# A packed second map in layer 0, its low part cut in three on VectorE, and other places for the degree counts

## The reference

```
x = layernorm(x + L0(x))     # L0: h = rmsnorm(x)*w; c = h@W_root + b + sum_r mean_r(h[src]@W_rel[r]);  r = 0, 1;  286 columns
                             #     L0 = x + elu(c) @ wo,   wo is 286 x 1024
x = layernorm(x + L1(x))     # L1: u = x@root + b + sum_r mean_r(x[src]) @ weight[r];  r = 0..7;  1024 x 1024 each
                             #     z = [u, x] @ w_gate + b;  L1 = tanh(u)*z + x*(1-z)
```

## Time and profile before

| | before |
|---|---|
| time, three runs | 837.8 us median (837.72 to 839.01) |
| profiled execution, its own time | 838.67 us |
| its span in the trace | 836.9 us |
| PE busy | 818.8 us, 98% |
| DVE busy | 672.2 us, 80% |
| ACT busy | 438.3 us, 52% |
| granted TensorE clock | 0.999 |

### The profile page before, as it was taken

How to read it: one execution, slowest core, us unless ns; L and a number is a source line. 1 busy time by engine, 2 the same in 40 slices (tenths; PEclk the granted TensorE clock), 3 DMA queues, 4 the chain that set the end, 5 groups by cost and what they waited for, 6 DMA issues and landing times.

```text
span 836.9 us, 15905 instructions
## 1 busy us (share of the span) xinstructions
PE 818.8 (98%) x6326; PEld 586.5 (70%) x6326; DVE 672.2 (80%) x969; ACT 438.3 (52%) x606; POOL 14.3 (2%) x32
## 2 busy tenths in 40 slices
PE   6999999999999999999999999999999999999996
PEld 5566744458877868768677686776867868778544
DVE  8999698998978677687776777767678676788997
ACT  5888558376556254453554535535456254444711
POOL 1000000000000000000000000000000000000000
PEclk9999999999999999999999999999999999999999
DMA  9411369202220220202202112021120220305711
GB/s 314 111 31 27 128 226 223 105 1 101 102 101 1 101 102 1 100 3 97 100 0 100 30 70 100 0 100 58 42 100 0 100 91 11 126 2 152 201 51 73
DMA packets 60125, 70.82 MB, mean 85 GB/s; under 512 B 30663, under 2 KB 34371, under 8 KB 60084
## 3 DMA queue, kind: packets, MB, share of 16 engines
q1 hardware_dynamic: 59207, 69.39, 26.2%
q10 hardware_dynamic: 876, 0.85, 0.4%
HBM read 57.71 MB, written 5.18 MB: 75 GB/s over the span
## 4 chain that ended last, share of the span: by engine, by line
PE 89%; DVE 6%; ACT 3%; DMA 1%; issue 1%; SPq 0%; DVEq 0%; ACTq 0%
PE psP L1162 51%; PE psA L1233 21%; PE psP L982 12%; PE psA L971 2%; PE psP L1086 1%; PE psP L942 1%; ACT cu_mem L676 1%; DVE p_mem L1463 1%; PE psP L991 1%; DVE vec L1384 1%; ACT wsplit L709 1%; DVE p_mem L1462 1%; DMA stage<-in_src 1%; ACT dump L596 0%; DVE wsplit L1410 0%
## 5 line engine op out<-in xcount | busy, mean ns | idle before, releaser
L1162 PE MATMUL psP<-wsplit,xT 128*128 128x256 f16 x2592 | 294.6, 273 | 0.0
L1162 PEld LDWEIGHTS psP<-wsplit,xT 128*128 128x128 f16 x2592 | 253.6, 98 | 33.0
L1233 PE MATMUL psA<-p_mem,cu_mem 128*128 128x512 f16 x800 | 175.3, 379 | 0.0
L1162 PE MATMUL psP<-wsplit,x 128*128 128x256 f16 x1296 | 150.3, 273 | 0.0
L1233 PEld LDWEIGHTS psA<-p_mem,cu_mem 128*128 (+1 forms) x800 | 78.2, 98 | 91.1 <-DVE cu_mem L1722 0.3
L1162 PEld LDWEIGHTS psP<-wsplit,x 128*128 128x128 f16 x1296 | 126.8, 98 | 14.6
L1424 DVE SCALAR_TENSOR_TENSOR wsplit<-stage,sc,wsplit 128x1024 f16<-128x1024 f32 x90 | 114.7, 1279 | 26.9 <-ACT wsplit L671 26.9
L671 ACT ACTIVATE wsplit<-stage,sc 128x1024 f16<-128x1024 f32 x90 | 100.6, 1137 | 16.6 <-DVE sc L1302 10.6
L1722 DVE SCALAR_TENSOR_TENSOR cu_mem<-psA,coef,cu_mem 128x512 f32<-128x512 f32 x80 | 60.0, 750 | 31.4 <-PE psA L1233 30.0
L671 ACT ACTIVATE wsplit<-x,sc 128x1024 f16<-128x1024 f32 x54 | 61.8, 1144 | 41.6 <-PE psP L1162 31.0
L1424 DVE SCALAR_TENSOR_TENSOR wsplit<-x,sc,wsplit 128x1024 f16<-128x1024 f32 x54 | 69.2, 1282 | 10.2 <-ACT wsplit L671 9.8
(11 more groups left out here) (211 smaller groups left out, 791.8 us busy)
## 6 DMA issues: line engine op xcount, KB each, us to landing
stage<-in_L_gnn_weight SPq DMA_DIRECT2D x16, 2048.0 KB, 7.8
stage<-in_L_gnn_w_gate SPq DMA_DIRECT2D x4, 2048.0 KB, 8.1
x_home<-x SPq DMA_DIRECT2D x5, 512.0 KB, 3.8
x<-x_home SPq DMA_DIRECT2D x5, 512.0 KB, 5.6
x<-in_x SPq DMA_DIRECT2D x4, 512.0 KB, 9.0
xT<-in_L_gnn_root SPq DMA_DIRECT2D x1, 2048.0 KB, 9.0
stage<-in_L_gnn_root SPq DMA_DIRECT2D x1, 2048.0 KB, 8.3
out<-x SPq DMA_DIRECT2D x4, 512.0 KB
```

Source lines behind the costliest of these rows:

```text
L1162: last = nc.tensor.matmul(psP[:, bank, (col + tt) * FB:(col + tt + 1) * FB], lhs[tt](a, c), split_block(n, b)[:, c, :], start=(first and t ...
L1233: last = nc.tensor.matmul(psA[:, (NT * h + t) % 2, :], cnt8[:, r, s, t * P:(t + 1) * P], p_part[h][a][:, s, :], start=(s == 0 and a == 0), ...
```

## The change

- wo's last chunk has only 30 rows. It is now packed: the rows are loaded three times, at partitions 0, 32 and 64 (three DMAs); wo's high part keeps all three, and its low part overwrites partitions 32 to 63. y's columns 256 to 285 are written three times at the same distances, and after the transposes y's low part overwrites partitions 64 to 93. So one matmul with 96 rows gives the three products of the chunk: 7 matmuls for a half and not 9 (`packed_product`).
- `wo_high` and `wo_low` go by chunks (three instructions each), `wo_low` now stands ahead of the layer 0 coefficients on DVE, and wo's scale ahead of the last `first_sums`. The second half of root, which waits for `wo_lo`, may load from then on.
- y's scaling goes from DVE (L1612, one a tile) to ACT (`y_scaled`, two a tile), with a shift from DVE. Row factors are made for tiles 0 and 1, 2 and 3, and 4, in three groups and not two. `y_low` is two instructions a tile and not one.
- On PE the degrees of layer 1 are counted in two pieces of 100: ahead of `wo_product(0)` and behind `root_product(0)`. `turn_y` of tiles 0 and 1 stands in the middle of `aggregate0` of tile 4. `aggregate0(0)` waits for the last sums only at its last source tile.
- Banks: three of the ten `wo_product` halves go elsewhere (halves 7 and 8 to psA), and `root_product(t)` writes bank (t + 3) % 5, the ones whose adds come first.
- On DVE root's low blocks 0 to 2 and 3 stand ahead of `x1_low(0)`, and `y_low(4)` and `wo_add(1, 0)` behind it. On ACT `y_high(4)` stands behind the first square root.

```
         def wo_bank(n):
+            return (psP[:, n, :] if n < NT else
+                    (psP[:, 0, :], psP[:, 1, :], psA[:, 1, :], psA[:, 0, :], psP[:, 2, :])[n - NT])
+        def root_bank(t):
+            return psP[:, (t + 3) % NT, :]
...
-            sp.dma_start(st_wo[0:F - (FC - 1) * P, FC - 1, :], wo_d[(FC - 1) * P:F, :]).then_inc(wo_tail_loaded, 16)
+            for q in range(3):
+                sp.dma_start(st_wo[q * QUAD:q * QUAD + FREST, FC - 1, :], wo_d[(FC - 1) * P:F, :]).then_inc(wo_tail_loaded, 16)
...
-            sp.wait_ge(wo_lo, 1)
+            sp.wait_ge(wo_lo, FC)
             load(U_ROOT + 1, 1, by_chunk(root_d[:, HALF:D]))
...
+            def y_scaled(t):
+                act.wait_ge(y_factors, t // 2 + 1)
+                last = elu_tmp[:, t, F - FREST:F].unsqueeze(1).broadcast_to([P, 2, FREST])
...
+                nc.scalar.activation(twice, last, ACT.Identity, bias=y_shift[:, t:t + 1], scale=rows_f[:, 0, 2, t:t + 1])
+                nc.scalar.activation(acc0[:, t, 0:F], elu_tmp[:, t, :], ACT.Identity, bias=y_shift[:, t:t + 1],
+                                     scale=rows_f[:, 0, 2, t:t + 1]).then_inc(y_ready, 1)
-            for t in range(NT - 1):
-                elu_exponential(t)
+            elu_exponential(0)
+            elu_exponential(1)
+            weight_sum(U_ROOT, 0, slot_load(U_ROOT), parts=(0,))
+            y_scaled(0)
+            y_scaled(1)
+            elu_exponential(2)
+            elu_exponential(3)
             y_high(0)
             y_high(1)
-            weight_sum(U_ROOT, 0, slot_load(U_ROOT), parts=(0, 1))
+            weight_sum(U_ROOT, 0, slot_load(U_ROOT), parts=(1,))
+            y_scaled(2)
             elu_exponential(NT - 1)
+            y_scaled(3)
             weight_sum(U_ROOT, 0, slot_load(U_ROOT), parts=(2, 3))
+            y_scaled(4)
             y_high(2)
             y_high(3)
             raw_high(U_ROOT, 0)
-            y_high(4)
...
+            def packed_product(out, t, cols):
+                _, hi, lo = unit_weights(U_WO)
+                for c in range(FC - 1):
+                    for a, w, first in ((0, hi, c == 0), (0, lo, False), (1, hi, False)):
+                        nc.tensor.matmul(out, yT[:, a, c, bass.ts(t, P)], w[:, c, cols], start=first, stop=False)
+                return nc.tensor.matmul(out, yT[0:3 * QUAD, 0, FC - 1, bass.ts(t, P)], hi[0:3 * QUAD, FC - 1, cols],
+                                        start=False, stop=True)
...
+            WO_FREE = {NT: (wo_added, 1), NT + 1: (wo_added, 2), NT + 2: (y_lo, 4), NT + 3: (y_lo, 5), NT + 4: (wo_added, 3)}
...
             def y_low(t):
                 dve.wait_ge(y_hi, t + 1)
-                tt(yT[:, 1, :, t * P:(t + 1) * P], psA[:, t % 2, 0:FPAD].rearrange("p (c n) -> p c n", c=FC),
-                   yT[:, 0, :, t * P:(t + 1) * P], ALU.subtract).then_inc(y_lo, 1)
+                nodes, third = slice(t * P, (t + 1) * P), slice(2 * QUAD, 3 * QUAD)
+                tt(yT[:, 1, 0:FC - 1, nodes], psA[:, t % 2, 0:FPAD - P].rearrange("p (c n) -> p c n", c=FC - 1),
+                   yT[:, 0, 0:FC - 1, nodes], ALU.subtract)
+                tt(yT[third, 0, FC - 1, nodes], psA[third, t % 2, FPAD - P:FPAD], yT[third, 0, FC - 1, nodes],
+                   ALU.subtract).then_inc(y_lo, 1)
...
             wo_add(0, 0)
+            unit_scale(U_ROOT, 0)
             wo_add(0, 1)
-            raw_low(U_ROOT, 0, (0, 1))
+            y_low(2)
+            y_low(3)
+            raw_low(U_ROOT, 0, (0, 1, 2))
             x1_factors(0)
+            raw_low(U_ROOT, 0, (3,))
+            x1_low(0)
             y_low(4)
             wo_add(1, 0)
-            x1_low(0)
             wo_add(1, 1)
-            raw_low(U_ROOT, 0, (2, 3))
             x1_factors(1)
```

More of the change, by code:

```diff
@@ L632, in wo_high @@
                 act.wait_ge(w_used, 1)
-                st, hi, _ = flat_weights(U_WO)
-                nc.scalar.activation(hi, st, ACT.Copy, scale=sc_f[:, scale_col(U_WO, 1), 2:3]).then_inc(wo_hi, 1)
+                st, hi, _ = unit_weights(U_WO)
+                for c in range(FC):
+                    nc.scalar.activation(hi[:, c, :], st[:, c, :], ACT.Copy,
+                                         scale=sc_f[:, scale_col(U_WO, 1), 2:3]).then_inc(wo_hi, 1)
             def weight_sum(i, slot, loads, parts=range(4)):
@@ L651, in weight_sum, with raw_high @@
                                          accum_out=am[:, slot, n:n + 1]).then_inc(wsum_ready, 1)
-            def raw_high(i, slot):
+            def raw_high(i, slot, blocks=range(4)):
                 act.wait_ge(scale_step, 4 * i + 4)
-                for n, (k, f) in enumerate(RAW):
+                for n in blocks:
+                    k, f = RAW[n]
                     b = weight_blocks(i) + n
@@ L963, in count_any, with product @@
                             quad(b, q0 + p, False)
-            def product(out, lhs, i, t, cols, part=None):
+            def product(out, lhs, i, t, cols, part):
                 _, hi, lo = unit_weights(i)
-                chunks = FC if i == U_WO else DC
-                for c in part or range(chunks):
+                for c in part:
                     for a, w, first in ((0, hi, c == 0), (0, lo, False), (1, hi, False)):
                         last = nc.tensor.matmul(out, lhs[:, a, c, bass.ts(t, P)], w[:, c, cols],
-                                                start=first, stop=(c == chunks - 1 and a == 1))
+                                                start=first, stop=(c == DC - 1 and a == 1))
                 return last
+            def packed_product(out, t, cols):
[5 more added lines that the diff above has]
+                                        start=False, stop=True)
             def raw_product(out, lhs, i, t):
@@ L1581, in _ @@
                 onehot_any()
-            unit_scale(U_WO, 1)
+            for c in range(FC):
+                wo_low(c)
             dve.wait_ge(deg0_full, 1)
@@ new lines, in y_factor @@
+            def y_factor(t0, t1):
+                tiles = slice(t0, t1)
+                dve.wait_ge(elu_done, t1)
+                step(nc.vector.tensor_reduce(rowmax[:, 0, tiles], elu_tmp[:, tiles, :], AX.X, ALU.max))
+                row_scales([rows[:, 0, a, tiles] for a in range(4)], rowmax[:, 0, tiles].bitcast(I32), least=127)
+                ts(y_shift[:, tiles], rows_f[:, 0, 2, tiles], -1.0, None, ALU.mult).then_inc(y_factors, 1)
+                ts(cy[:, tiles], rows_f[:, 0, 3, tiles], sc_f[:, U_WO, 3:4], 0.5, ALU.mult, ALU.mult).then_inc(cy_ready, 1)
```

107 lines of the change are left out of this document (58 added, 49 removed).

## The result

| | before | changed |
|---|---|---|
| time, 11 runs each | 837.84 us median (837.66 to 839.01) | 840.19 us median (838.97 to 841.58) |
| ratio of medians | 1 | 1.0026, 95% interval 1.0017 to 1.0035 |
| profiled execution: time, span, clock | 838.67, 836.9, 0.999 | 838.99, 837.2, 0.996 |

Slower by 0.26%, where 2.7 us (0.3%) faster were forecast. Two differences must be explained: the profiled execution is 0.3 us slower, not 2.7 faster, and the median is 1.2 us above that execution. Four of the 11 executions took 838.97 to 839.32 us, with a clock of 0.996 over the whole run, and seven 840.08 to 841.58, with 0.994 or 0.992.

What follows compares the result with a forecast made beforehand. Bound: PE, busy 98%, with a close race of PE, DVE and ACT ahead of its unbroken run. The second root tile starting at 132.0, not 134.69, gives 2.7 us off the 837.8 median: 835.1, range 833.9 to 837.2.

Steps and rivals of the forecast that it cites:

- PE's work: Second map on PE: ten halves lose 2 matmuls each at 0.2156 us, 20 matmuls or 4.31 us.
- the sentence on the degrees: PE, layer 1 degrees: still 200 matmuls at 0.0252 us, 5.0 us, half of them now following the first root tile.
- ScalarE: Rival: ACT's scaling pairs step by 2.3 us, ACT becomes the bound, kernel slower at 841.2; chance 0.04.
- wo's split: ACT and DVE before layer 0 coefficients: 3.33 us leave DVE's path at 100.34, coefficients start 1.15 later, at 92.4.
- The scaling on ACT: y's scaling: DVE loses five at 0.367; ACT gains pairs of 0.63 and 0.43, stepping by 0.88, 4.4 us for five.
- The layout up to root tile 1: Hand-laid order of PE, ACT and DVE: second root tile starts at 132.0 instead of 134.69, 2.7 us gained.
- Layer 1 takes it over: After the root tiles: layer 1 keeps the 2.7 us lead, for which DVE must itself be 1.2 earlier.
- Given back in the chain: Rival: ACT and DVE chain, 107 to 128 us, gives most back; gain 0.9, 836.9; chance 0.20.
- root's second load: Rival: the load issued at 92.4 shares the first one's bandwidth, holding the first scaling; gain 1.7, 836.1; chance 0.03.
- the cheap matmul: Rival: removed matmuls cost 131 ns rather than 216, so the saving is 1.7 less, 836.8; chance 0.01.

Runs made afterwards that it cites:

- spread kernel: Changed kernel with only its degree matmuls moved on TensorE, into pieces of 50, 50 and four of 25 in place of two blocks of 100; median 837.26 us, ratio 0.9991.
- one slower record: The changed kernel itself, unaltered, profiled a second time; one execution, 840.81 us at a clock of 0.992.
- the filler: Changed kernel with the later 100 degrees moved ahead of tile 4 and 12 unused 512-column matmuls behind root tile 0; median 838.93 us, ratio 1.0010.

## Why the prediction was wrong

- **PE's work.** The matmul price was right, 7 matmuls a half at 0.2156, the 96-row one the same: a half steps by 1.52, 7 times 0.217. What was wrong is the sentence on the degrees. I priced 100 of them at 0.0252 each, 2.5 us, which is what the block took, and took its place behind root tile 0 as free but for that, in the gap ahead of tile 1. It cost 1.7 us more on the 216 matmuls behind it (48.47 us for 46.78), which the forecast took to run as before ("the same layer 1 from there"). **This is the step that failed**: the working has no term for the clock, though the order showed the degrees gathered from pieces of at most 75 into two of 100. No rival had it either, so the chance of slower (0.03) stood on ScalarE alone. The spread kernel shows its size: of the 5.1 us between 835.1 and 840.2, 2.9 go with the places of the degrees. Of these, 1.7 are the low stretch behind the later block. The other 1.2, the step from the profiled execution to the median, fit the stretch behind the wait in tile 4, which one slower record shows (in the spread kernel degrees fill that wait); that this holds for all seven slower executions is not shown. Of the other 2.2, 1.3 are the layout's (below), and 0.9 the step from the profiled time to the median, which I took over from before (838.67 to 837.8) and which the spread kernel doesn't have (837.25 and 837.26).
- **wo's split.** Right, and 0.8 to 1.0 us earlier than laid out: DVE's lows 87.8 to 91.6 (forecast 88.8 to 92.4), coefficients at 91.63 rather than 92.4, PE waits of 0.66 and 1.42 (0.7 and 1.5).
- **The scaling on ACT.** Right: 0.43 and 0.61 (0.43 and 0.63). The Trainium skill's page "ScalarE: Activation LUTs" (section "What ACT_TABLE_LOAD costs") has the price from which the prediction's estimate of 0.42 and 0.61 is worked out; the rows agree with it. The 32-row low part took 0.29 (0.28). The two pieces run one behind the other, 0.75 a tile. I had put the second piece at +0.1 a tile and then left it out of the layout, which has 0.55 for the step: 0.2 late in tile 4.
- **The layout up to root tile 1.** 1.3 us late, 133.28 for 132.0. Most of it, 0.9, goes back to one place: I had `x1_high(0)` end at 118.3, and it ended at 119.19. ACT waited 0.76 for the shift, because the factors stand behind three low blocks on DVE (until 116.4, the rows above); I had laid out those blocks as done by 117.2 (they were at 117.95) without asking what stands behind the third. The 0.2 of `y_low(4)` comes to it. From there the lateness stayed near 1.1: factors 125.3 (124.2), `x1_low(1)` 128.38 (127.3). The last 0.2 are the transpose, which landed 3.55 us after its issue and not 3.14. PE's wait in tile 4 grew from 1.7 to 2.85 but was not what set root tile 1 in this execution: the spread kernel fills it, and root tile 1 waits 1.95 us for its transposed tile there. `y_low(4)` and `wo_add(1, 0)` ahead of `x1_low(0)` bring 1.64 us (133.28 to 131.64), the same 1.64 by which `x1_low(1)` comes earlier, which shows that DVE's chain did; some 0.3 of it, my estimate from the two records counted from 98 us, are the first one's low stretch at 105.6.
- **Layer 1 takes it over.** Right: it keeps the lead. In the spread kernel 1.4 us at root tile 1 are 1.4 of the profiled time (838.67 to 837.25).
- **The rivals.** "Given back in the chain" was half of what happened (gain 1.4 of 2.7 before the clock). ScalarE, root's second load and the cheap matmul did not come. The form of "slower" that did come was not among them.

The change's own parts are small beside this: packing 0.4 to 1.0 us. With the degrees spread the whole change is worth 0.8 us at the median (its interval ends at no change), and 2.4 with `x1_low(0)` moved behind `y_low(4)` and the residual add.

## What to carry to other kernels

Small matmuls put in a block as a cheap filler are not free of charge: ask what clock the wide work behind them gets, and read the granted clock by stretches before believing a PE that looks 100% busy. Keep such work in small pieces between wide matmuls; where a wait can't be avoided, don't put them next to it (25 of them and a wait of 1.68 us were once enough here). When laying out an order by hand, write down for every short instruction on which another engine waits what stands ahead of it in its queue.

## What the hardware showed that was not expected

- A low stretch here cost 1.7 us of wide work where it lay on wide work alone. It started at the end of a block of 100 one-column matmuls (up to 0.1 us before it) or up to 1.2 us behind; with 200 it started 1.1 us before the end and still cost 2.8 (216 matmuls in 49.61 us for 46.78).
- A DMA transpose of 128 x 1024 took 3.55 to 4.43 us to land with a block of 100 one-column matmuls beside it, and 3.04 to 3.06 without; why is open.
- Low clock did not lengthen one-column matmuls: the last 40 or so of the 200 ran at the same 0.025 us each at a clock of 0.50.
- Executions of one kernel differ in which stretches are low. The mean clock of a run (0.996, 0.994, 0.992) counts them, but not what they cost: the execution with the later block in the wait of tile 4 took 838.40 us at 0.994, and one with the filler 838.58 us at 0.997.
